# One-hots with the key inside the value and permutation and plan among the placing steps, in a two-layer graph kernel

## The reference, cut to what is computed

```python
def _L0_gnn_ref(h, relvectors, w_ih, w_hh, b_ih, b_hh, edge_src, edge_dst, edge_rel):
    msg = h[edge_src] + relvectors[edge_rel]
    red = jax.ops.segment_sum(msg, edge_dst, num_segments=h.shape[0])
    return _gru_cell(red, h, w_ih, w_hh, b_ih, b_hh)

def _L1_gnn_ref(x, W, edge_index):          # self loops are added to edge_index
    deg = jax.ops.segment_sum(jnp.ones_like(src, dtype=x.dtype), src, num_segments=N)
    deg_rsqrt = jax.lax.rsqrt(deg)
    vals = deg_rsqrt[src] * deg_rsqrt[dst]
    h = x @ W.T
    return jax.ops.segment_sum(vals[:, None] * h[dst], src, num_segments=N)

x = _layernorm(x + _L0_gnn_ref(x, ..., src, dst, edge_type_16))
x = _layernorm(x + _L1_gnn_ref(x, L1_gnn_W, jnp.stack([src, dst])))
```

## Time and profile before

| | us |
|---|---|
| median of three runs | 2451.86 (2450.61 to 2453.98) |
| the profiled execution | 2450.72 |
| its span, first to last instruction | 2448.7 |

### The profile page before, as it was taken

One profiled execution on the slowest core, in us unless ns is written; L12 is line 12 of the kernel. 1 busy time (PEld: TensorE's weight loads), 2 busy tenths in 40 slices (PEclk: granted clock), 3 DMA queues, 4 the chain that ended last, 5 costly groups with the idle time before them and its releaser, 6 DMA issues.

```text
span 2448.7 us, 43994 instructions
## 1 busy us (share of the span) xinstructions
PE 2001.0 (82%) x10013; PEld 1548.1 (63%) x10013; DVE 1745.1 (71%) x2996; ACT 831.4 (34%) x3093; POOL 1628.2 (66%) x1767
## 2 busy tenths in 40 slices
PE   2489898879989769999997589888888888877773
PEld 2366666657666547777774477767676777665552
DVE  5678787788868668888875577767784787544674
ACT  4000000023323226767654366516560665200002
POOL 3677777777777745655510577777777777777774
PEclk7699999989989879999999699999999999999997
DMA  3244444444444335444442433333333333333334
GB/s 97 84 123 149 140 148 143 146 127 149 144 139 145 112 104 148 145 137 141 141 124 79 141 106 107 105 105 106 106 105 105 106 106 105 105 106 106 104 105 149
DMA packets 131522, 296.52 MB, mean 121 GB/s; under 512 B 31024, under 2 KB 64914, under 8 KB 131304
## 3 DMA queue, kind: packets, MB, share of 16 engines
q0 software_dynamic: 80016, 219.06, 31.0%
q10 hardware_dynamic: 35100, 57.62, 7.2%
q1 hardware_dynamic: 16188, 17.21, 2.2%
HBM read 260.91 MB, written 32.85 MB: 120 GB/s over the span
## 4 chain that ended last, share of the span: by engine, by line
PE 34%; POOL 26%; issue 14%; ACT 8%; DMA 8%; DVE 6%; DVEq 1%; SPq 1%; POOLq 0%; ACTq 0%
POOL rows L540 25%; PE ps L1542 19%; ACT rows L1333 6%; DMA rows<-gdram,ids 6%; PE ps L1639 4%; PE ps L1680 3%; DVE rows L700 3%; PE ps L1699 2%; PE ps L1682 2%; PE ps L1671 1%; SPq L398 1%; ACT sums L1482 1%; PE ps L1606 1%; DVEq L761 1%; PE ps L1669 1%
## 5 line engine op out<-in xcount | busy, mean ns | idle before, releaser
L1542 PE MATMUL ps<-rows,onehot 128*128 x5632 | 1372.2, 400 | 206.2 <-SPq L389 124.2
L1542 PEld LDWEIGHTS ps<-rows,onehot 128*128 128x128 f32 x5632 | 1085.8, 197 | 434.3 <-issue 256.2
L540 POOL DMA_INDIRECT rows<-in_x_dram,ids x832 | 796.5, 957 | 344.8 <-issue 245.0
L540 POOL DMA_INDIRECT rows<-gdram,ids x832 | 788.8, 948 | 246.7 <-issue 212.4
L796 DVE TENSOR_TENSOR sums<-sums,ps 128x256 f32 x400 | 168.2, 420 | 332.4 <-PE ps L1542 323.0
L1333 ACT ACTIVATE rows<-rows,a 128x128 f16<-128x128 f16 x624 | 190.8, 388 | 365.7 <-DVE rows L700 365.7
L766 DVE SCALAR_TENSOR_TENSOR onehot<-tkey,node_p,ps 128x512 f32<-128x512 f32 x403 | 298.4, 741 | 13.4 <-issue 10.2
L813 DVE TENSOR_TENSOR sums<-ps,sums 128x800 f16<-128x800 f32 (+1 forms) x156 | 216.3, 1414 | 1.3 <-issue 1.3
L706 DVE SCALAR_TENSOR_TENSOR onehot<-tkey,node_p,ps 128x1024 f32<-128x1024 f32 x154 | 195.7, 1271 | 1.4 <-issue 1.3
L1333 ACT ACTIVATE rows<-rows,b 128x128 f16<-128x128 f16 x624 | 189.5, 386 | 0.0
L1280 ACT COPY sums<-ps 128x256 f32<-128x256 f32 x49 | 18.2, 372 | 502.9 <-PE ps L1598 491.6
(11 more groups left out here) (271 smaller groups left out, 1875.3 us busy)
## 6 DMA issues: line engine op xcount, KB each, us to landing
xpd<-sums ACTq DMA_DIRECT2D x48, 384.0 KB
sums<-xpd ACTq DMA_DIRECT2D x48, 384.0 KB, 3.9
rows<-in_x_dram,ids POOLq DMA_INDIRECT x832, 2.8
rows<-gdram,ids POOLq DMA_INDIRECT x832
xt<-in_x_dram ACTq DMA_DIRECT2D x96, 128.0 KB, 2.2
gdram<-sums ACTq DMA_DIRECT2D x48, 128.0 KB, 1.8
out_dram<-sums SPq DMA_DIRECT2D x6, 896.0 KB
sums<-gdram SPq DMA_DIRECT2D x4, 896.0 KB
```

The lines of the kernel that those rows point to most:

```text
L540: pool.indirect_dma_start(rows[:, at:at + D], None, source, bass.IndirectOffsetOnAxis(ap=ids[:, p, s * h + k:s * h + k + 1], axis=0)).then ...
L1542: prod = M.matmul(ps[:, h, 0:width], onehot[:, u % U, k, :], rows[:, bass.ds(at + k * stride, width)], start=(k == 0), stop=(k == q - 1))
```

## The change

It has four parts.

1. **Layout and operands of the one-hots.** A table `iota_k` in SBUF (128 x 208 x 8, f16) holds each value 8 times in a row. The keys of the second sort are kept as f16 (`lo_16`, `hi_16`). A one-hot now has the key inside the value: for value 0 the 8 (or 16) keys, then for value 1. All three operands are f16 in SBUF with step 1 inside. TensorE and ScalarE read one key's one-hot with a step: 16 bytes in a batch, 32 in a counting round. The same one-hots serve the second layer's batches.
2. **Counting and closing.** The 52 rounds of counting stand in 45 steps (8 to 52), closing and the first places in steps 53 and 54.
3. **Placing.** Steps 55 to 106 have the placing rounds. The plan is cut into pieces at steps 56 to 62, the split of places into 13 pieces from step 60, and 24 of the 26 batches of chunk 0 stand in steps 63 to 111, a pair of steps each, in three buffer sets. x's transposes go to bank 2 in place of bank 7, which the permutation now uses. The node steps keep two batches.
4. **GpSimd.** The gather of the second layer is written chunk by chunk; the first index copy of each chunk is made when the chunk begins.

The diff, cut to its core:

```diff
+COUNTING = 45
+CLOSE = FIRST + COUNTING
+PLACE = CLOSE + 2
+PLAN = PLACE + 1
+PERMUTE = PLACE + 8
+BATCHES = (WIN - PERMUTE) // 2
+SPLIT_LAG = 5
+QUAD = SUB // CH * 4
...
+        iota_k = sb("iota_k", [P, G, PB], F16)
...
-        oh_lo = early(2, SUB, P, dt=F16)
-        oh_hi = early(2, SUB, B, dt=F16)
+        oh_lo = early(2, P, SUB, dt=F16)
+        oh_hi = early(2, B, SUB, dt=F16)
...
+        planned = again(0, 3 * C)
...
+        planned = again(begin_b, begin_b + SUB * P // 2)
...
+        perm0 = [perm_set(hots_a, hots_a), perm_set(free, again(end_a - C, end_a)), perm_set(hots_c, hots_c)]
+        seen = free(2, SUB // 2 * B, dt=F16)
+        lo_16 = again(end_a - C, end_a)(C, dt=F16)
+        hi_16 = again(end_a - 2 * C, end_a - C)(C, dt=F16)
+        floor4 = free(CH, QUAD)
...
+        def counted(j):
+
+            return range((j - FIRST) * RND // COUNTING, (j - FIRST + 1) * RND // COUNTING)
...
+            for _ in range(S1):
+                pool.sem_inc(s_free[1], 1)
+            turns = NG1 // S1
+            for g in range(CH):
+                a = g * turns
+                stage(1, S1 * H1, s_tix, a, a % 2)
+                with pool.Fori(0, turns // 2) as i:
+                    for p in range(2):
+                        issue(1, gdram[:, :], S1, H1, D, s_tix, i * 2 + (a + p), (a + p) % 2)
+                issue(1, gdram[:, :], S1, H1, D, s_tix, a + turns - 1, a % 2, False)
...
-                floor_of(hi1, lo1, P)
-                step(V.scalar_tensor_tensor(lo1, hi1, -float(P), lo1, ALU.mult, ALU.add))
+                floor_of(mask, lo1, P)
+                step(V.tensor_copy(hi_16, mask))
+                step(V.scalar_tensor_tensor(a32[:, :], mask, -float(P), lo1, ALU.mult, ALU.add))
+                step(V.tensor_copy(lo_16, a32[:, :]))
+                note(V.tensor_copy(iota_k[:, :, :], iota[:, 0:G].rearrange("p (a k) -> p a k", k=1).to_broadcast([P, G, PB])))
...
-                    out_ap, ps[:, 6, 0:width].rearrange("p (a v) -> p a v", a=1).to_broadcast([P, count, width]),
-                    keys.rearrange("p (k a) -> p k a", a=1).to_broadcast([P, count, width]), ALU.is_equal)
+                    out_ap, iota_k[:, 0:width, 0:count],
+                    keys.rearrange("p (v k) -> p v k", v=1).to_broadcast([P, width, count]), ALU.is_equal)
...
                 return V.tensor_tensor(
-                    out_ap.rearrange("p (g i) v -> p g i v", g=CH),
-                    ps[:, 6, 0:width].rearrange("p (g i v) -> p g i v", g=1, i=1).to_broadcast([P, CH, each, width]),
-                    now.rearrange("p g (i v) -> p g i v", v=1).to_broadcast([P, CH, each, width]), ALU.is_equal)
+                    out_ap.rearrange("p v (g i) -> p v g i", g=CH),
+                    iota_k[:, 0:width, 0:each].rearrange("p (v g) i -> p v g i", g=1).to_broadcast([P, width, CH, each]),
+                    now.rearrange("p (v g) i -> p v g i", v=1).to_broadcast([P, width, CH, each]), ALU.is_equal)
...
-                round_hots(oh_lo[:, h], lo1, r, P).then_inc(s_deg_oh, 1)
-                round_hots(oh_hi[:, h], hi1, r, B).then_inc(s_deg_oh, 1)
+                round_hots(oh_lo[:, h], lo_16, r, P).then_inc(s_deg_oh, 1)
+                round_hots(oh_hi[:, h], hi_16, r, B).then_inc(s_deg_oh, 1)
...
-                hots = oh_hi[:, h].rearrange("p (a s) b -> p a (s b)", a=2)
+                hots = oh_hi[:, h].rearrange("p b (a s) -> p a b s", a=2)
+                seen_v = seen.rearrange("p a (b s) -> p a b s", b=B)
                 dve.wait_ge(s_run, r + 1)
                 dve.wait_ge(s_seen, r + 1)
-                V.tensor_tensor(seen, seen, hots, ALU.add).then_inc(s_seen, 1)
+                V.tensor_tensor(seen_v, seen_v, hots, ALU.add).then_inc(s_seen, 1)
                 settle()
                 dve.wait_ge(s_part, r * (SUB // 2) + SUB // 2)
-                V.tensor_tensor(prod, hots, ps[:, 4:6, 0:SUB // 2 * B], ALU.mult).then_inc(s_prod, 1)
+                V.tensor_tensor(prod.rearrange("p a (b s) -> p a b s", b=B), hots,
+                                ps[:, 4:6, 0:SUB // 2 * B].rearrange("p a (b s) -> p a b s", b=B), ALU.mult).then_inc(s_prod, 1)
                 dve.wait_ge(s_prod, r + 1)
                 each = SUB // CH
                 note(V.reduce_sum(
                     pos.rearrange("p (g w) -> p g w", g=CH)[:, 0:CH // 2, bass.ds(r * each, each)],
-                    prod[:, 0, :].rearrange("p (g i b) -> p g i b", g=CH // 2, b=B), axis=AX_X))
...
+            def split_places(k):
+
+                def cells(a):
+                    return a.rearrange("p (g w) -> p g w", g=CH)[:, :, k * QUAD:(k + 1) * QUAD]
+
+                settle()
+                dve.wait_ge(s_part, (k * 4 + 5) * (SUB // 2))
+                step(V.tensor_scalar(floor4, cells(pos), -(P - 1) / 2, 1.0 / P, ALU.add, ALU.mult))
+                step(V.tensor_scalar(floor4, floor4, MAGIC, None, ALU.add))
+                step(V.tensor_scalar(cells(n16[:, :]), floor4, MAGIC, None, ALU.subtract))
+                step(V.scalar_tensor_tensor(cells(m16[:, :]), cells(n16[:, :]), -float(P), cells(pos),
+                                            ALU.mult, ALU.add))
+
+            def chunk_columns():
+
+                for g in range(1, CH):
                     part = slice(g * G, (g + 1) * G)
-                    note(V.tensor_scalar(n16[:, part], mask[:, part], float(g * G), None, ALU.subtract))
...
+            def x_part(j):
+
+                t = (j - FIRST) // 2
+                if (j - FIRST) % 2 and t < NT:
+                    k = t % 2
+                    dve.wait_ge(s_xps[k], (t - k) * 8 + 16)
+                    add_x_part(t, k)
...
+            def placing_step(j):
+
+                r = j - PLACE
+                if r < RND:
+                    places(r, r % 2)
+                if r < RND - 1:
+                    buckets_of(r + 1, (r + 1) % 2)
+                if j == PLAN:
+                    plan_columns()
+                if j == PLAN + 1:
+                    degree_roots()
+                if j == PLAN + 2:
+                    plan_nodes()
+                if j == PLAN + 4:
+                    plan_groups()
+                if j == PLAN + 6:
+                    plan_releases()
+                    dve.sem_inc(s_pp, 2)
+                if r >= SPLIT_LAG and (r - SPLIT_LAG) % 4 == 0 and r < SPLIT_LAG + RND:
+                    split_places((r - SPLIT_LAG) // 4)
+                if j == WIN - 2:
+                    chunk_columns()
+                if j >= PERMUTE:
+                    q = (j - PERMUTE) // 2
+                    if (j - PERMUTE) % 2 == 0 and q < BATCHES:
+                        offset_hots(q)
+                    elif (j - PERMUTE) % 2:
+                        bucket_hots(q)
+                x_part(j)
+
+            walk(FIRST, CLOSE, counting_step)
+            walk(CLOSE, PLACE, closing_step)
+            walk(PLACE, WIN, placing_step)
...
+            dve.wait_ge(s_pp, BATCHES + 2)
...
-                tiles = node_beside(u, u, tiles, (u, u) if u < 2 else None, u < U - 1)
+                tiles = node_beside(u, u, tiles, BATCHES + u if u < 2 else None, u < U - 1)
...
-                    tiles = node_beside(i * W8 + (U + u), u, tiles, batch_at(i, u), u < W8 - 1)
+                    tiles = node_beside(i * W8 + (U + u), u, tiles, None, u < W8 - 1)
...
-                    A.activation(dump[:, q, :], prod[:, 1, q * B:(q + 1) * B], ACT.Identity,
+                    A.activation(dump[:, q, :], prod[:, 1, :].rearrange("p (b s) -> p s b", b=B)[:, q, :], ACT.Identity,
...
+            for j in range(FIRST, WIN):
+                t, odd = (j - FIRST) // 2, (j - FIRST) % 2
+                if 0 <= j - PLACE < RND:
+                    half_places(j - PLACE)
+                if odd and t + 1 < NT:
+                    copy_x(t + 1)
+                    if t + 3 < NT:
+                        load_x(t + 3, (t + 3) % 2, P if t + 3 < NT - 1 else LAST)
+                if j >= PERMUTE and (j - PERMUTE) // 2 < BATCHES:
+                    scaled((j - PERMUTE) // 2, (j - PERMUTE) % 2)
+                if odd and t < NT:
+                    store_x(t, t % 2, P if t < NT - 1 else LAST)
...
-                        A.activation(dest[:, k, :], slot[0][:, k, :], ACT.Identity,
+                        A.activation(dest[:, k, :], slot[0][:, :, k], ACT.Identity,
...
-                node_beside(u, u, 0, (u, u) if u < 2 else None, False, (u - 1, u - 1) if 0 < u < 3 else None)
+                node_beside(u, u, 0, BATCHES + u if u < 2 else None, False, BATCHES + u - 1 if 0 < u < 3 else None)
...
-                    node_beside(i * W8 + (U + u), u, i * 2 + u // U, batch_at(i, u), True, batch_at(i, u - 1))
+                    node_beside(i * W8 + (U + u), u, i * 2 + u // U)
...
-                    last = M.matmul(ps[:, 4 + a, z:z + B], oh_lo[:, h, q, :], oh_hi[:, h, q, :],
+                    last = M.matmul(ps[:, 4 + a, z:z + B], oh_lo[:, h, :, q], oh_hi[:, h, :, q],
...
```

(28 more changed lines are left out.)

352 lines of the change are left out of this document (139 added, 213 removed).

## The result

The changed kernel takes **2954.62 us** (median of 4 runs, 2953.60 to 2960.70), the kernel before 2451.24 us beside it: a ratio of **1.206, 95% interval 1.204 to 1.208**. The profiled execution has a span of 2951.9 us. I predicted 2463 us with a range of 2408 to 2503: the sign is right, the size is far off, by 492 us.

A forecast was written before the change was run, and what follows sets the result against it. GpSimd's issue was taken to bound counting, placing and the second layer, TensorE the node steps. Terms -27 - 33 + 5 + 24 + 13 + 29 = +11 us, with 2450.7 and 1.1, gave 2463 us, range 2408 to 2503.

The forecast's parts named there:

- Strided reads: TensorE's stepped reads in batches and counting rounds: 0 us taken; at the other end twice the time, 1.39 us more per batch.
- The slack argument: Second layer: three steps and a slow batch need 8.2 us of TensorE, the gathers 8.2, so slow reads cost up to 25 us.
- Placing: Placing steps: 51 bucket one-hots and 24 batches hold GpSimd's gathers, +13 us (4 to 25).
- The hole: Gap between the last placing eviction and the next: shrinks by 27 us (20 to 33), from 45.4 to 18 us.
- The node steps: Node steps, bound by TensorE: 24 of 26 permutation batches leave, saving 33 us (30 to 45); steps of 8.8 us.
- The plan: Plan among the placing steps: VectorE falls behind and GpSimd is blocked, +5 us (0 to 15).
- counting: Counting: 52 rounds of one-hots with two SBUF inputs hold gathers, 0.47 us each, +24 us (6 to 54).
- What the new layout takes back: One-hots with both inputs in SBUF hold gathers: +24 us in counting, +13 in placing, +29 in the second layer.
- the formula: Hold of the gathers: a VectorE instruction with two SBUF inputs, L us long, costs (L - 0.17)^2 / 2.5 us.
- The port costs little: Rival, chance 0.26: held gathers cost little and the first layer's gain stays, -60 + 15 = -45 us, 2408 us.
- Slow stepped reads: Rival, chance 0.16: stepped reads by TensorE and ScalarE are slow, +11 plus 20 to 40 us, 2483 to 2503.
- Doubled rate doesn't set in: Rival, chance 0.03: VectorE's one-hots stay at 2.3 and 1.9 us but hold gathers as well, about 2640 us.

The follow-up runs named there:

- g1: The changed kernel with ScalarE's offsets' one-hots in fours (8 bytes a step) and TensorE's columns' one-hots in pairs (4 bytes): 2491.75 us, 1.016 of the kernel before.

## Why the prediction was right or wrong

- **"Strided reads": the step that failed.** I took 0 us for TensorE's stepped reads and bounded the other end at twice the time, 1.39 us more a batch. The trace of before had no stepped read, and I had no reason for the 2. Measured is 4.2 times the time of a matmul (0.364 us for 0.088), 4.4 us more a batch. And the bound left out the clock: with the fall behind each batch the three walk steps go from 5.4 to 7.3 us.
- **The slack argument fell with it.** I compared 3 x 1.82 + 2.8 = 8.2 us of TensorE with the 8.2 of the gathers. TensorE needed 13.16 us (315.8 us for 24 times three steps, 190.0 before): 5.24 a batch, and 72 of them are 377 of the second layer's 401 us. The comparison was the right one, only a hair from tipping; the term in it deserved a wider bound, since everything beyond 2.8 goes to the time undiminished.
- **"Placing" +13 was +123.** TensorE is busy 439.4 us of 440 there (558 to 998 us), and 24 batches at 4.4 us more are 106 us; what the clock adds (0.86 in this stretch, 0.95 before) and what slack takes off isn't taken apart. GpSimd waits 80 us for free rows between 484 and 1000 us, 0.9 in the placing steps before: that too was among my signs of being wrong. In g1, with pairs, the stretch costs 21.
- **"The hole" 18 us was 25.9** (21.0 in g1). The mechanism was right; the chain of the node tiles and the loads took VectorE's 18.33 us of waiting in place of my 11, the rest was 6.4 of the 6.9 foreseen.
- **"The node steps" 8.8 us were 9.10**: the two batches left there cost 6 us each. In g1 they are 8.77.
- **"The plan" and counting** together +18.7 of +29 up to step 63. Counting is the hold about as foreseen: from 160 to 440 us GpSimd starts 210 gathers for 224, waits for free rows 1.5 us in all, and is busy 1.03 us a gather for 0.95. TensorE was close behind, which I had not seen: its counting round, with weights and columns every 32 bytes, takes 1.74 us in place of 0.57, and it is busy 299 of 300 us.
- **"What the new layout takes back", second layer +29**: 31.6 us of longer gathers, 820.4 for 788.8. The size was right, but it was hidden behind TensorE in the changed kernel. It decides only in g1, and there the 76 us that the formula gives for its longer one-hots were 51 in the gathers and 57 in the stretch.
- **The rivals.** The port costs little: no, as g1's 51 us show. Its price was also added up wrong: my own terms give -60 + 5 = -55 us, not -60 + 15. Slow stepped reads, the one with 0.16: the right mechanism, priced at 20 to 40 us where the smaller steps of g1 took back 463. Of the signs I had named for it both are there, slow batches on TensorE and VectorE's waits: 733 us for the walk matmuls behind them (1470 to 2670 us). Doubled rate doesn't set in: it did, within 12 ns of what I had worked out (1228, 570, 696, 1020).
- **The sign came out right by luck, in the main.** I forecast "slower" because of the held gathers, and in the changed kernel's second layer they were hidden behind TensorE. g1 shows what my mechanism is worth without the slow read: the kernel is some 40 us slower than before, the moves' gain already taken off.

What stays open: why rows came late in four groups, and whether it was the rows; what in the slow read pulls the clock; why the 16-bit counting gains there; and why, there, the batches' iota in SBUF made placing (63 to 111) shorter, 400 us, than the iota in PSUM, 466, though VectorE's instructions take equally long.

## What to carry to other kernels

A layout has a reader for every writer: before turning one to please VectorE, price the same tile as a moving operand, and take the bound of a read that no trace shows from its bytes, not from "twice". Here two keys inside a value were all but free for TensorE, eight were four times as slow and slowed the work behind them by the clock. And an f16 table in SBUF in place of PSUM is no gift where GpSimd's gathers are the bound: such an instruction holds a gather that starts beside it.

## What the hardware showed that I had not expected

- TensorE's moving operand of f16, 208 columns: 0.088 us contiguous, 0.091 at 4 bytes a step, 0.183 at 8, 0.364 at 16, at a granted clock of 1.00. At 0.50 a contiguous batch of 16 goes from 1.60 to 2.95 us; the ones at 8 and 16 bytes stay at 3.13 and 6.03.
- The granted clock fell to 1.2 GHz some 4 us into most batches with 16-byte steps (in some 6) and came back some 5 us behind it; the walk behind batches of 4 and 8 bytes a step kept its pace, as it did behind 6.2 us of contiguous matmuls; and the fall came only behind every second batch when the batches were cut in halves of 2.9 us.
- ScalarE's f16 read of 128 elements: 388 ns at 2 and 4 bytes a step, 396 at 8, 506 at 16.
- VectorE reached its doubled rate with four keys in a row and not with two: 128x1664 in 1.02 us with 8 and with 4, 1.64 with 2, 1.89 with the key repeated along the run.
- Adding 52 short matmuls to a batch brought 324 pauses of up to 2.5 us between single matmuls, 251 us in all, that no releaser explains.
